# Expert attention: which engine issues the load of the spread queries and keys

## The reference, cut to what matters

```python
def expert_step(acc, params):
    q = (x @ qw.T + qb_).reshape(B, S, H, Dh).transpose(0, 2, 1, 3)
    k = (x @ kw.T + kb_).reshape(B, S, H, Dh).transpose(0, 2, 1, 3)
    v = (x @ vw.T + vb_).reshape(B, S, H, Dh).transpose(0, 2, 1, 3)
    scores = jnp.einsum('bhqd,bhkd->bhqk', q, k) * scale
    p = jax.nn.softmax(scores, axis=-1)
    o = jnp.einsum('bhqk,bhkd->bhqd', p, v)
    o = o.transpose(0, 2, 1, 3).reshape(B, S, E) @ ow.T + ob_
    return (acc + o * g[..., None], None)
```

## Time and profile before

| | |
|---|---|
| median of 3 runs | 2469.64 us |
| span of the profiled execution (the page gives no other time of it) | 2469.5 us |
| PE busy, of the span | 1995.8 us, 81% |
| DVE busy | 1761.0 us, 71% |
| ACT busy | 1453.6 us, 59% |
| POOL busy | 1028.3 us, 42% |
| mean granted clock of PE | 0.908 |

### The profile page before, as it was taken

The page is one execution under the profiler, slowest core; times in us unless marked ns, Lnnn a source line. Parts: engine busy times, 40 slices in busy tenths (PEclk is TensorE's granted clock), DMA queues, the critical chain, the costliest instruction groups (busy, mean ns, idle before and its releaser), DMA issues. The chain is left out here.

```text
span 2469.5 us, 52904 instructions
## 1 busy us (share of the span) xinstructions
PE 1995.8 (81%) x18992; PEld 926.7 (38%) x18992; DVE 1761.0 (71%) x3039; ACT 1453.6 (59%) x2138; POOL 1028.3 (42%) x1009
## 2 busy tenths in 40 slices
PE   5647888888888888888847988988988988888886
PEld 3421222222222222222223554654554554555454
DVE  4736666676666666666658978878878877887794
ACT  4313556666555656555726766756757657666573
POOL 0011111111111111111039968858758767686680
PEclk9856889999899999888969998999999999999998
DMA  1022222222222222222010000000000000000000
GB/s 32 2 52 51 45 54 55 47 51 49 44 52 56 52 56 52 56 52 54 2 58 1 2 29 10 12 30 10 12 31 10 12 30 10 12 30 11 12 2 10
DMA packets 52105, 77.07 MB, mean 31 GB/s; under 512 B 10899, under 2 KB 45749, under 8 KB 48053
## 3 DMA queue, kind: packets, MB, share of 16 engines
q1 hardware_dynamic: 51317, 74.06, 13.0%
q10 hardware_dynamic: 576, 0.15, 0.0%
HBM read 47.70 MB, written 25.69 MB: 30 GB/s over the span
## 5 line engine op out<-in xcount | busy, mean ns | idle before, releaser
L902 DVE TENSOR_REDUCE ENM<-PM 128x1 f32<-128x512 f32 x1024 | 656.5, 685 | 335.9 <-PE PM L735 328.4
L832 ACT ACTIVATE EPT<-PA 128x1024 f32<-128x1024 f32 x512 | 520.0, 1021 | 212.0 <-PE PA L747 199.9
L735 PE MATMUL PM<-EKX,EQX 48*128 48x512 bf16 x1024 | 359.7, 414 | 177.0 <-DMA EKX<-e_park 91.0
L1216 POOL TENSOR_TENSOR DRN<-DRN,DHALF 128x8 f32<-128x8 f32 x192 | 364.5, 1899 | 7.4
L655 POOL CAST ENMP<-ENM 128x16 bf16<-128x16 f32 x64 | 12.6, 196 | 847.8 <-DVE ENM L902 847.8
L1214 POOL TENSOR_TENSOR DQR<-DR 128x512 f32<-128x512 f32 x192 | 244.2, 1272 | 246.9 <-DVE DR L1497 245.5
L735 PEld LDWEIGHTS PM<-EKX,EQX 48*128 48x128 bf16 x1024 | 83.6, 95 | 585.4 <-DVE ENM L902 404.1
L757 PE MATMUL PV<-EPT,EVP 128*32 128x512 f32 x2048 | 295.2, 651 | 0.9 <-ACT EPT L832 0.7
L747 PE MATMUL PA<-EQX,EKX 51*128 51x512 bf16 x1024 | 263.2, 404 | 5.2 <-DMA EQX<-EROWS 4.9
L1259 PE MATMUL PM<-DWQKV,DXS 128*128 128x512 f32 x384 | 216.6, 647 | 39.5 <-ACT XNT L1456 23.2
L1495 DVE TENSOR_TENSOR DR<-DRAW,DTAB 128x512 f32<-128x512 f32 x192 | 193.1, 1005 | 61.9 <-POOL DQR L1219 28.2
(11 more groups left out here) (204 smaller groups left out, 2930.8 us busy)
## 6 DMA issues: line engine op xcount, KB each, us to landing
e_park<-EPARTS SPq DMA_DIRECT2D x64, 192.0 KB, 2.9
EQX<-e_park SPq DMA_DIRECT2D x32, 384.0 KB, 5.6
EKX<-e_park SPq DMA_DIRECT2D x32, 384.0 KB, 9.2
DWQKV<-in_WqkvR SPq DMA_DIRECT2D x6, 1536.0 KB, 6.3
e_park<-EPARTS SPq DMA_DIRECT2D x64, 128.0 KB, 2.6
e_park<-EPARTS SPq DMA_DIRECT2D x64, 64.0 KB, 2.1
EQX<-EROWS SPq DMA_DIRECT2D x256, 3.0 KB
DWO<-in_WoR SPq DMA_DIRECT2D x6, 512.0 KB, 4.3
```

The lines of the kernel that those rows point to most:

```text
L735: pe.matmul(PM[:, r, :], lhsT=QX[64 * r:64 * r + KQ, b, hp, t * 128:(t + 1) * 128], rhs=KX[64 * r:64 * r + KQ, b, hp, :], start=True, stop ...
L832: s_.activation(PT[:, kt, pair * 2 * S:(pair + 1) * 2 * S], PA[:, 2 * pair:2 * pair + 2, :].rearrange("p a b -> p (a b)"), ACT.Exp, scale= ...
L902: v.tensor_reduce(NM[:, g % 2, t, j, 0:1], PM[:, r, :], AX.X, ALU.max, negate=True).then_inc(maxed, 1)
L1216: g.tensor_tensor(rn, rn, HALF[:, 0:8], ALU.pow).then_inc(rooted.sem, 1)
```

## The change

The four DMAs of the bulk load are issued by POOL in place of SP. In the program of POOL they stand in the first slot of each half, directly behind the splitting of the queries and keys, with two waits ahead of them: for `kscored`, as SP's writes have it, and for all 12 writes (`parked`). In the program of SP they stood in the second slot, behind the rows. SP keeps the writes, the rows and the loads of weights. For the first half, POOL issues the load between its splitting and the fill of the value tile.

```diff
@@ SP
-                def bring_in(e, b):
-                    sp.wait_ge(parked, (e * B + b) * PARK + PARK)
-                    for i, dst in enumerate((QX, KX)):
-                        for r in range(2):
-                            sp.dma_start(dst[64 * r:64 * r + KQ, b, :, :].rearrange("p h n -> p (h n)"),
-                                         park[b, i, r].rearrange("t (d h) n -> (t d) (h n)", d=DH)).then_inc(spread, 16)
...
-                    if "v" in uses:
-                        eb, gb = ahead(e, g, HG)
-                        bring_in(eb, gb // HG)
...
-                sp.wait_ge(keys_set, 1)
-                bring_in(0, 0)
@@ POOL
+                def bring_in(e, b):
+                    pool.wait_ge(parked, (e * B + b) * PARK + PARK)
+                    pool.sem_inc(pool_passed, 1)
+                    for i, dst in enumerate((QX, KX)):
+                        for r in range(2):
+                            pool.dma_start(dst[64 * r:64 * r + KQ, b, :, :].rearrange("p h n -> p (h n)"),
+                                         park[b, i, r].rearrange("t (d h) n -> (t d) (h n)", d=DH)).then_inc(spread, 16)
...
                     if "q" in uses:
                         eb, gb = ahead(e, g, HG)
                         split(eb, gb // HG, use(e, g, "q"))
+                        if not (first and g == 0):
+                            pool.wait_ge(kscored, (e * NG + g) * 8)
+                            pool.sem_inc(pool_passed, 1)
+                        bring_in(eb, gb // HG)
 
                 split(0, 0, 1)
+                pool.wait_ge(keys_set, 1)
+                bring_in(0, 0)
```

## The result

| | before | after |
|---|---|---|
| median, us (4 runs each) | 2470.51 | 2440.38 |
| lowest to highest, us | 2464.82 to 2473.20 | 2438.51 to 2443.81 |
| ratio, 95% interval | 1 | 0.9877 (0.9857 to 0.9897) |
| span of the profiled execution, us | 2469.5 | 2442.0 |
| mean granted clock of PE | 0.908 | 0.915 |

The change makes the kernel 1.2% faster, by 30 us. I had forecast 2476 us and no change.

What follows compares the result with a forecast made beforehand. TensorE's wait for the bulk load of spread queries and keys, with its slow clock, was taken as the bound. 15 x (8.4 - 8.1) + 2 for the first load = +6.5 us on 2469.6: 2476 us, range 2400 to 2520.

Steps and rivals of the forecast that it cites:

- a load which comes in time could give at most 121 us: Spread wait in 15 later halves: 4.79 us of wait plus 3.3 us of slow clock each, 121 us in all.
- the price c: Time that one DMA issue holds GpSimd, four ahead of the maxima's split in each half: taken as 0.9 us.
- the 3 us that I had named as a sign of being wrong: Sign: the forecast is wrong if GpSimd's four issues take under 3 or over 4.2 us.
- my own formula: Added wait at the turn of the maxima: 0.6 + 4c, forecast as 4.2 us with c at 0.9.
- The park is complete 9.4 us after its first write: Writes ahead of the bulk load: complete at 754.0, so the load can start 5.0 us earlier.
- The clock's term: Slow clock behind the new wait at the maxima: 3.3 us mean share plus 0.9 for the values' projection, 4.2 us.
- the old loss: Spread wait and its slow clock in the kernel before: 8.1 us per half.
- my own case: Wait moves from spread to maxima with about the same loss, c 0.8 to 1.0: 2468 to 2484 us, chance 0.33.
- rival A: Cheap GpSimd issue, c about 0.42: added wait 2.3 us, middle loss 4.4 us per half, 2414 us; chance 0.29.
- the rows as covered: Next group's rows in each half: landed at 765.6, needed about 770; only some 1.5 us to spare under rival A.

Runs made afterwards that it cites:

- 8 issues: The changed kernel with each of GpSimd's four DMAs cut into two of half the columns; 2472.91 us, ratio 1.0021 to the kernel before.
- queries' pair by GpSimd: Against the kernel before: GpSimd issues the queries' two loads behind its splitting, the sync engine the keys' two behind the rows; 2423.34 us, ratio 0.9822.
- load early, by the sync engine: The kernel before with all four loads issued by the sync engine behind the writes, ahead of the second slot's rows; 2477.29 us, ratio 1.0031.
- load early, by GpSimd behind the maxima: The changed kernel with its load moved from behind the splitting to behind the second slot's split of the maxima; 2476.40 us, ratio 1.0027.

## Why the prediction was wrong

| kernel | wait per half | half | half - 56.6 - wait |
|---|---|---|---|
| before | 4.79 (spread) | 64.50 | 3.1 |
| 8 issues | 5.27 (maxima) | 64.10 | 2.2 |
| after | 3.2 (maxima) | 62.45 | 2.6 |
| queries' pair by GpSimd | 2.24 (maxima) | 61.38 | 2.5 |
| load early, by the sync engine | 4.25 (rows) | 65.06 | 4.2 |
| load early, by GpSimd behind the maxima | 4.48 (rows) | 64.91 | 3.8 |

The last column is what a half loses beside its wait. That this is the clock's doing, and that 56.6 is the right base, the changed kernel shows by itself. Its waits are 2.9 to 3.2 us in all halves but the first of the 15, and the halves sort by how long the clock stood at 0.50: with some 3 us of it three halves took 60.8 to 61.3 us, with some 7 us six took 62.3 to 62.6, with some 10 us four took 63.4 to 63.5. So each further 3 us or so at the low clock cost 1.0 to 1.4 us. Carried on to no fall at all, a half would take 59.9 us, which is an estimate: 56.7 and the wait of 3.2.

**What was right.** That the load had to start earlier and that this removes the whole wait for the spread; that the wait moves to the turn of the maxima, in all 15 halves, released by GpSimd's last subtraction; that the transfer is as fast from GpSimd, the rows nearly in time (they kept PE 0.2 to 0.4 us in three halves), and the clock falls again. Of the Trainium skill's section Issuing engines are not separate DMA queues (DMA: Bandwidth & Descriptors), the part that the same DMA engines move the data held here: 5.7 and 9.4 us to landing against 5.6 and 9.2. The step "a load which comes in time could give at most 121 us" is borne out too: 15 x (64.50 - 56.6) = 118.

**The step that failed first is the price c,** "I take the mean of its cast and its two-operand pass ... and c = 0.9". An issue takes (1.05 + 1.03) / 4 = 0.52 us, near the sync engine's 0.42 and far from a pass over a tile. The four take 2.08 us, under the 3 us that I had named as a sign of being wrong, and the 8-issue run shows that an issue does not go by bytes. An instruction that moves no tile through the engine had no business with the duration of one that does; the row of the same DMA on another queue was nearest, and I had it as the lower bound only. The 1 us to the first byte of the Trainium skill (DMA: Bandwidth & Descriptors, Specifications) was not what an issue holds the engine either. By my own formula 0.6 + 4 x 0.52 = 2.7 us; the wait was 3.2.

**"The park is complete 9.4 us after its first write"** was 0.6 us short for GpSimd: 744.69 - 734.70 = 9.99 us. That is the missing 0.5 of the wait. The row had it for SP, and I carried it over to another engine's queue. At the same place, the start of the stage, GpSimd issues 182.95 - 173.01 = 9.94 us after the first write, where SP had 9.40; why, no run shows:

```profile
182.95 1.25 POOL L644 DMA_DIRECT2D EQX<-e_park  x2 [6.17 <-issue]
```

The two errors, -1.5 and +0.5, together make 4.2 predicted against 3.2 measured.

**The clock's term failed with the same weight: 4.2 us per half instead of 2.6.** I had added the values' projection whole at the low clock, to a share taken from two of the old waits. The fall comes near the end of the new wait and is over sooner than the old one. At the maxima the share hardly goes by the wait's length: 2.5, 2.6 and 2.2 us at 2.24, 3.2 and 5.27 us. It goes more by where the wait stands: 3.1 us at the spread, and 3.8 to 4.2 us at the rows, though these waits were shorter than 4.79 us. I had carried the share of one place over to another.

With these the sum comes out: 3.2 + 2.6 = 5.8 us per half against 7.9, 15 x -2.1 = -31, and +3 for the first load. The shares are taken from these same halves, so this shows where the error lay and is no test of the terms. My forecast had 8.4 against 8.1, +6.5 us. Of the 35 us in between, 15 x 1.5 = 23 are the price c and 15 x 1.6 = 24 the clock's term; the park, 8 us, and the old loss, 7.9 instead of 8.1, go the other way. With only one of the two put right, the sum would have been some 17 us faster. The time lay inside the range, between my own case and rival A (2414), whose condition, c under 0.8, was met. A's middle was too low since it gave a wait of 2.3 us a fall in half of the cases, and at 2.24 us it came in all 15; the park's 0.5 us were missing in it as well.

**What I had not seen:** I listed the rows as covered by some 4 us, by 1.5 us if the issue were cheap, and left it there. They are covered only because the new wait holds PE back. Take the new wait away, as the two early loads did, and the rows become a wait of 4 to 5 us that costs more than the change gives. The sync engine's issues are cheaper than GpSimd's and gained nothing by starting early. What gained was the order of 8 DMAs on its queue: two loads, four rows, two loads.

## What to carry to other kernels

Before a late transfer is moved forward, look at the small, urgent ones that share the DMA engines with it: put just as much of the bulk in front of them as ends before they are needed, and the rest behind. Work queued behind a DMA wait on an in-order engine is part of the price of that wait, so look for an engine with nothing due, or put the wait behind what is due. And price an issue by the nearest issue, not by the engine's other work.

## What the runs showed of the hardware that I had not expected

- A plain DMA of 48 rows holds GpSimd 0.52 us, with 384 KB as with 192 KB.
- Small copies waited for a bulk in front of them even when the two went by different queues: 72.1 us in 17 waits, against 68.6 in one queue and 4.9 in 2 before. From 762 to 768 us nothing at all moved on the copies' queue.
- GpSimd went on 9.94 us after the park's first write was issued, the sync engine 9.40 us, both at the start of the stage.
- TensorE's clock went to 0.50 at, or up to 2 us behind, all 15 waits of 1.9 to 3.2 us at the maxima (mean 2.24), and behind none of 13 waits of 0.83 to 0.98 us at the same place; behind a second wait of 1.0 to 1.4 us in the same half it fell in four halves, and these took 4 to 5 us more than the eight without a fall. In one pair of halves a fall cost 2.1 us (60.3 against 62.4 us).
